# Causal stage of a four-layer transformer kernel: ScalarE issues the small transfers of the turned row maxima, which SyncE issued

## What is computed

```python
qkv = (x @ Wqkv_w + Wqkv_b).reshape(Bb, Ll, 3, Hh, dd)
q, k, v = ...                                   # each [batch, 16 heads, 1024, 8]
scores = jnp.einsum('bhid,bhjd->bhij', q, k) * scale
causal_mask = jnp.triu(jnp.full((Ll, Ll), -10000.0, dtype=scores.dtype), 1)
attn = jax.nn.softmax(scores + causal_mask, axis=-1)
y_softmax = jnp.einsum('bhij,bhjd->bhid', attn, v)
...
def step(state, inp):
    q_t, k_t, v_t = inp
    state = retention * state + Gamma * (v_t[..., :, None] * k_t[..., None, :])
    y_t = jnp.einsum('bhij,bhj->bhi', W_static + state, q_t)
    return (state, y_t)
...
y = alpha * y_softmax + (1.0 - alpha) * y_stp
return y @ out_w + out_b
```

## Time and profile before

| | us |
|---|---|
| median of 3 runs (1801.25 to 1804.1) | 1802.07 |
| the profiled execution | 1806.19 |
| its span in the trace | 1804.9 |

### The profile page before, as it was taken

How to read it: one execution, slowest core, us unless ns; L and a number is a source line. 1 busy time by engine, 2 the same in 40 slices (tenths; PEclk the granted TensorE clock), 3 DMA queues, 4 the chain that set the end, 5 groups by cost and what they waited for, 6 DMA issues and landing times. The chain is left out here.

```text
span 1804.9 us, 45554 instructions
## 1 busy us (share of the span) xinstructions
PE 1556.2 (86%) x19648; PEld 998.5 (55%) x19648; DVE 1275.3 (71%) x2003; ACT 1098.3 (61%) x1641; POOL 697.8 (39%) x499
## 2 busy tenths in 40 slices
PE   3587897899999999999977778888788888899999
PEld 2354566787778778877863232433333343466565
DVE  4656644777777677768767868778777886655665
ACT  3255576777767777786752567677667767533331
POOL 4122300554255344534450556365465545411100
PEclk8789898999999999999997889999999999999999
DMA  7864200000000000000024274246237222223332
GB/s 176 196 165 113 47 5 12 2 2 2 2 2 2 2 1 2 2 1 2 32 88 99 52 212 98 63 133 142 56 107 167 66 64 72 67 71 94 95 96 76
DMA packets 54821, 121.17 MB, mean 67 GB/s; under 512 B 6124, under 2 KB 14468, under 8 KB 53020
## 3 DMA queue, kind: packets, MB, share of 16 engines
q1 hardware_dynamic: 51708, 112.74, 23.7%
q10 hardware_dynamic: 2912, 5.51, 1.8%
HBM read 85.70 MB, written 31.74 MB: 65 GB/s over the span
## 5 line engine op out<-in xcount | busy, mean ns | idle before, releaser
L1445 DVE TENSOR_REDUCE arena<-ring 128x2 f32<-128x1024 f32 (+2 forms) x320 | 342.1, 1110 | 87.9 <-PE ring L1302 62.1
L1545 ACT ACTIVATE arena<-ring 128x1024 f32<-128x1024 f32 (+1 forms) x320 | 291.3, 937 | 135.4 <-PE ring L1331 92.0
L1352 PE MATMUL accs<-arena 128*9 128x512 f32 (+3 forms) x1536 | 174.3, 528 | 3.8 <-ACT arena L1545 3.8
L2509 POOL TENSOR_TENSOR arena<-arena 128x1280 f32<-128x1280 f32 x28 | 65.3, 2332 | 287.0 <-PE accs L2270 231.7
L1295 PE MATMUL ring<-arena 48*128 48x512 bf16 (+3 forms) x768 | 128.8, 347 | 41.8 <-DVE arena L1445 21.1
L1324 PE MATMUL ring<-arena 51*128 51x512 bf16 (+3 forms) x768 | 125.0, 343 | 45.8 <-DVE arena L1445 25.1
L2501 POOL TENSOR_TENSOR arena<-arena 128x512 f32<-128x512 f32 x112 | 141.3, 1294 | 3.0 <-DVE arena L2311 3.0
L287 POOL TENSOR_SCALAR xn<-x,moments,rstd 128x128 f32<-128x128 f32 x80 | 65.0, 825 | 192.3 <-DVE rstd L258 178.3
L2782 ACT ACTIVATE arena<-ring 128x512 f32<-128x512 f32 x80 | 47.7, 596 | 134.8 <-PE ring L2651 132.7
L2494 POOL TENSOR_TENSOR arena<-arena 128x1024 f32<-128x1024 f32 x32 | 86.3, 2698 | 108.1 <-DVE arena L2368 108.1
L1718 POOL TENSOR_TENSOR arena<-arena 128x1024 f32<-128x1024 f32 x28 | 65.9, 2354 | 128.6 <-ACT arena L1558 104.5
(11 more groups left out here) (342 smaller groups left out, 4165.9 us busy)
## 6 DMA issues: line engine op xcount, KB each, us to landing
arena<-whole_k SPq DMA_DIRECT2D x32, 512.0 KB, 4.6
arena<-whole_q SPq DMA_DIRECT2D x32, 512.0 KB, 6.2
arena<-moe_scratch SPq DMA_DIRECT2D x128, 128.0 KB, 2.9
arena<-c_scratch_q SPq DMA_DIRECT2D x14, 384.0 KB, 9.3
arena<-c_scratch_k SPq DMA_DIRECT2D x14, 384.0 KB, 12.2
a_scratch_k<-arena SPq DMA_DIRECT2D x8, 512.0 KB, 4.2
c_scratch_k<-arena SPq DMA_DIRECT2D x8, 512.0 KB, 4.5
arena<-a_scratch_q SPq DMA_DIRECT2D x9, 384.0 KB, 7.2
```

What stands on the lines that cost most here:

```text
L1352: mm = nc.tensor.matmul(acc[ci % 2][32 * h:32 * h + HD + 1, a - c * BANK:BANK], c_values[b % 2][:, j, r * HEADS // 2 + 2 * g + i, :], weig ...
L1445: nc.vector.tensor_reduce(dst, src, AX.X, ALU.max, negate=True).then_inc(c_max_taken.up(item), 1)
L1545: nc.scalar.activation(view(c_probs[wi % 4]), view(ps), ACT.Exp).then_inc(c_weights_made.up(item), 1)
```

## The change

ScalarE's program waits, right behind its copy L1532, for that copy's own signal, and issues the four transfers itself. SyncE's branch for S goes. Nothing else differs; source, destination, sizes and signals of the transfers are the same.

```diff
                         nc.scalar.activation(c_neg_T[u % 2][:, cols], ps[0:SPLIT * GROUP, cols], ACT.Copy).then_inc(
                             c_neg_T_made.up((b, g, part)), 1)
+                        ac.wait_ge(c_neg_T_made, (b, g, part))
+                        for r in range(2):
+                            for p in range(2):
+                                first = (2 * r + p) * SPLIT
+                                nc.scalar.dma_start(cq_stack[b % 2][64 * r + SCORE:64 * r + SHIFT, 2 * g + p, cols],
+                                                    c_neg_T[u % 2][first:first + SPLIT, cols]).then_inc(
+                                    shift_signal(b, g, part).up((b, g, part), 16), 16)
                     elif kind == "W":
...
-                    elif kind == "S":
-                        _, b, g, part = item
-                        u = unit(b, g)
-                        cols = slice(*(P * n for n in max_parts(b, g)[part]))
-                        sp.wait_ge(c_neg_T_made, (b, g, part))
-                        for r in range(2):
-                            for p in range(2):
-                                first = (2 * r + p) * SPLIT
-                                nc.sync.dma_start(cq_stack[b % 2][64 * r + SCORE:64 * r + SHIFT, 2 * g + p, cols],
-                                                  c_neg_T[u % 2][first:first + SPLIT, cols]).then_inc(
-                                    shift_signal(b, g, part).up((b, g, part), 16), 16)
```

## The result

| | before | changed |
|---|---|---|
| median of 4 runs, us | 1801.66 (1797.6 to 1804.1) | 1846.65 (1844.99 to 1849.44) |
| the profiled execution, us | 1806.19 | 1847.27 |
| its span, us | 1804.9 | 1845.9 |

The ratio is 1.0257, with a 95% interval of 1.0239 to 1.0275: the changed kernel is slower by 45 us between the medians (46 by the ratio). The forecast was 1831, slower by 29, in a range to 1848. The direction, the stall and the steps behind it came true; the size was short by 16 us.

What follows compares the result with a forecast made beforehand. Bound: a TensorE, VectorE and ScalarE loop tied by three ring buffers. Losses 0 + 2.1 + 7.6 + 3.4 + 13.0 + 2.9 = 29.0 us; 1806.2 + 29.0 = 1835.2, less 4.1 for a median: 1831 us, range 1810 to 1848.

Steps and rivals of the forecast that it cites:

- the steps behind it: Behind an S copy: late exponential, late score on TensorE through three used-up ring buffers, VectorE's maxima some 2.9 us late.
- rival A: ScalarE hands each transfer over in 0.31 to 0.35 us, delay 1.5 us; 10 us lost, 1812 us; chance 0.18.
- do not agree: Claim that this transfer's rows, 0.66 us for 6 KB, contradict the skill page's "small" initiation time.
- the worked place: The S whose copy ends at 1387.79, followed in detail: ScalarE 2.98 us late, 2.6 us lost.
- I take half: Three S at a sequence's finish: half the overhangs of 0.95, 0.95 and 2.29 us lost, 2.1 us together.
- the eight places without slack: S copies with no ScalarE idle time behind them: 3.4, 13.0 and 2.9 us lost by class.
- the pass-through: How much of ScalarE's 2.98 us delay reaches VectorE through the ring buffers: 2.6 us at the worked S.
- The five: Five S without slack, like the one worked at 1387.79: 13.0 us lost together.
- the last: The S at 1520.9, followed by six exponentials without a gap: 2.9 us lost.
- rival B: Every overhang passes whole, 37.5 us, plus twelve V at TensorE's lower clock, 10.1; 48 us, 1850 us; chance 0.08.
- slow-V discount: S at 1087 and 1117, a 1.89 us V already behind: 2.6 less 0.9, 1.7 us lost each.
- Four fifths of the overhang: Four S with 0.49 to 0.73 us idle before the next exponential: 1.9 us lost each, 7.6 together.

## Why the prediction was right, and where it was short

**Right, and shown.** The issue's price: 0.66 taken, 0.682 measured; rival A's 0.31 to 0.35 is out. The Trainium skill says in "DMA: Bandwidth & Descriptors", section "Issuing engines are not separate DMA queues", that the time to initiate a DMA is usually small relative to the DMA itself. The traces show no landing time for this transfer, so they don't test that ratio; my "do not agree" was more than the rows gave. What they show is that four times 0.68 us is not small for the engine that issues. Four issues behind one wait made up the whole effect; a stall of that length without a transfer made the same. The delay: ScalarE's next instruction 2.98 later was the forecast; at the worked place the exponential starts 3.03 later relative to the copy (3.93 behind its start, 0.90 before), and the held-up score came at 5.00 for 5.08. SyncE's freed queue: 0 taken, and 0 shown by the run that kept its wait. GpSimd's fetches bring nothing: its busy time and place in the chain don't grow, and the freed queue gives nothing. The wait itself: nothing. The three places at a sequence's finish came out at 3.3 or 2.1 us for 2.1, but "I take half" had no row behind it, so that is luck.

**Short: the eight places without slack.** The step that failed is the pass-through, "I take 2.6 us lost" and its followers, 1.7 and 2.9. The five were 4.2 each, the two with a slow V 3.2, the last 5.9 to the end: 33.2 us for 19.3, and these 14 us are nearly all that the forecast lacks. As a loss of the ring alone 2.6 was about right: where TensorE stayed at its upper level, an interval of the shortest kind lost 2.4. What I left out of the sum is that TensorE, idle for 2.74 us, then ran at the lower level, V at 1.90 instead of 1.05; I had it in rival B, priced at 10.1 us, and gave that rival 0.08. The useless matmuls took 2.0 to 2.8 us off each of the three shortest intervals, and that is about what the forecast lacks there.

**Not owed: the slow-V discount.** I took 0.9 off at two places, because a V of 1.89 us stood there already. Against that one trace it looks right: they lost 3.0 and 3.4 where the intervals of the same kind lost 5.2 and 4.9, and 4.0 and 3.7. But the slow V belonged to that one execution. In the traces of the wait alone, of the spread issues and of the change only where there is slack, the V's right behind the copies at the same two places take 1.04 or 1.05 us, and the first of the two intervals is 28.9 us, not 30.3. Against the first two of these traces the two places lost 8.2 us for 3.4, the worst miss of all classes. A row seen in one execution was taken for a trait of the kernel.

**A little short: the places with slack.** "Four fifths of the overhang", 1.9 each; measured 2.9 in mean for those four against the trace before, 2.3 against the two traces without loss. The kernel that changed only the nine places with slack or in the first unit cost 11.2 by its times for 9.7, nearly as summed. In its own trace the same nine places cost 15.9 us, against 13.3 in the changed kernel's, so there is no sign that they cost more when the other eight have a stall as well.

**The sum.** Between the profiled executions the difference is 41.0, but there the changed kernel reached its first S 5.5 us sooner; from the first S on it is 46.5, and of the medians 45. Full pass-through, the 37.5 of rival B, with its clock term 10.1 is 48: the truth lies between the forecast and rival B, nearer B. The earlier trace rows had the clock at 0.93, already below full, and the earlier trace rows a V at the lower level behind an S. That was reason to put the term into the sum.

**What stays open.** The size of the clock's share. TensorE's matmuls between the first and last S took 23.0 us more, but part of that time is in waits that would be there anyway. The interval that was cleanest gives 2.8 of 5.2 us. At the eight places the trace with nine useless matmuls gives 8.9 us of 33.2, with five 11.2, and with five only there 4.6; the times of this last kernel give 10 us. Some 5 to 15 us, an estimate from these, is as close as the runs come. Executions of one and the same kernel point the same way, though not always: the ten with S two places later go from 1786.26 us at a mean granted clock of 0.959 to 1806.44 at 0.944, while thirteen of the kernel before, all within 5 us, show no such order. The gain of 1.6 us in the first unit and the first S 5.5 us earlier are not effects of the change: the kernel with the wait alone has 1.5 us and 11.6 us of the same in its trace.

## What to carry over

An engine with much idle time and a small share of the chain can still be where a stall hurts: look at what stands behind the new instruction in its queue and whether the ring buffers are used up at that moment. The DMA issues here cost nothing where each stood behind an exponential that ScalarE was working on, and held ScalarE for their whole length where they stood behind a wait for its own result; so spread them one behind each long instruction. Read a place in more than one trace before giving it a price of its own. And where TensorE is made to stand for some us again and again in a stage whose granted clock is already under 1.00, put its slower matmuls into the sum and not only into a rival.

## What the runs showed of the hardware that I had not expected

- ScalarE's queue issues a transfer in 0.68 us alongside an exponential of 1.02 us that has just started, at no cost that the time shows (ratio 0.9991); the same four in a row behind a wait cost 45 us over the stage.
- The same 5310 matmuls were busy for 460.1, 468.6, 480.0 and 486.0 us as ScalarE was held 0, 1.5, 2.4 and 2.8 us behind each copy, with a granted clock of 0.93, 0.91, 0.89 and 0.88. With short stalls of one engine, another engine's instructions took longer.
- Useless matmuls in the stall kept the V behind it at 1.05 us where it was 1.72 to 1.90: nine of them at all eight places without slack, five at seven of eight, and in another kernel's trace five at only three of eight. Eight such groups made the slower kernel's times shorter (1.0202 against 1.0257).
